# Decoder layer on one core: attention cut into two halves that run one batch apart, with the second recurrence of batch 0 ahead of the first of batch 1 in the prologue

## What is computed

```python
x = x + attn(layernorm(x))       # mix with the token before (tm_k, tm_v, tm_r); k, v, r = mixed @ Wk.T, Wv.T, Wr.T
                                 # out = (sigmoid(r) * layernorm(wkv(k, v))) @ Wo.T
x = x + wkv2(k=layernorm(x), v=ctx_2048)
x = x + ffn(layernorm(x))        # (silu(z @ gate.T * gs) * (z @ up.T * us)) @ down.T * ds, 1408 inner features
```

## Time and profile before

| | |
|---|---|
| time, median of 3 runs | 614.09 us (613.96 to 615.02) |
| time of the profiled execution | 616.2 us |
| its span in the trace | 614.2 us |
| busy: PE, DVE, ACT, POOL | 539.0, 460.5, 345.0, 47.9 us |
| granted clock of PE, mean | 0.945 |

### The profile page before, as it was taken

The page is one execution under the profiler, slowest core; times in us unless marked ns, Lnnn a source line. Parts: engine busy times, 40 slices in busy tenths (PEclk is TensorE's granted clock), DMA queues, the critical chain, the costliest instruction groups (busy, mean ns, idle before and its releaser), DMA issues.

```text
span 614.2 us, 8078 instructions
## 1 busy us (share of the span) xinstructions
PE 539.0 (88%) x2658; PEld 384.2 (63%) x2658; DVE 460.5 (75%) x727; ACT 345.0 (56%) x546; POOL 47.9 (8%) x155
## 2 busy tenths in 40 slices
PE   3998671269999997999999997999999997999995
PEld 2443331168447577997447477996447487999994
DVE  5899429928999459978999469968998479863343
ACT  4648447548546455758546365768556365763231
POOL 2000110012001110012001010012001010010000
PEclk9999695569999999999999998999999998999999
DMA  8999300010010000020020000030010000000001
GB/s 308 378 379 375 117 0 0 1 40 31 0 69 1 1 0 2 35 86 17 0 68 0 0 0 0 34 99 3 0 68 0 0 0 0 34 35 1 1 34 37
DMA packets 11877, 34.65 MB, mean 56 GB/s; under 512 B 912, under 2 KB 912, under 8 KB 11664
## 3 DMA queue, kind: packets, MB, share of 16 engines
q1 hardware_dynamic: 11856, 34.37, 15.3%
HBM read 30.18 MB, written 12.85 MB: 70 GB/s over the span
## 4 chain that ended last, share of the span: by engine, by line
PE 71%; DVE 12%; issue 6%; ACT 5%; POOL 2%; DMA 2%; SPq 0%; DVEq 0%; POOLq 0%; ACTq 0%
PE bank L473 27%; PE gu L557 19%; PE dacc L487 10%; PE bank L533 8%; PE bank L462 5%; DVE t_slot L773 2%; DMA t_xres<-in_x 2%; PE bank L510 1%; DVE t_stats L752 1%; DVE t_z L765 1%; POOL t_rstd L439 1%; ACT t_z L626 1%; DVE t_st L900 1%; ACT L580 1%; DVE t_slot L881 1%
## 5 line engine op out<-in xcount | busy, mean ns | idle before, releaser
L557 PE MATMUL gu<-t_z4h,t_gate 128*128 128x256 f32 x352 | 92.5, 294 | 15.0 <-DVE t_h L931 13.2
L557 PE MATMUL gu<-t_z4l,t_gate 128*128 128x256 f32 x352 | 90.5, 289 | 0.0
L557 PE MATMUL gu<-t_z4h,t_up 128*128 128x256 f32 x352 | 90.1, 288 | 0.0
L557 PE MATMUL gu<-t_z4l,t_up 128*128 128x256 f32 x352 | 89.9, 287 | 0.0
L557 PEld LDWEIGHTS gu<-t_z4h,t_gate 128*128 128x128 f32 x352 | 69.0, 196 | 19.1 <-DVE t_h L931 14.8
L697 ACT ACTIVATE t_h<-gu,t_fsc 128x256 f32<-128x256 f32 x88 | 40.2, 472 | 66.6 <-PE gu L557 62.1
L487 PE MATMUL dacc<-t_down,t_hh 128*128 128x512 f32 x176 | 73.3, 416 | 0.0
L557 PEld LDWEIGHTS gu<-t_z4l,t_gate 128*128 128x128 f32 x352 | 69.1, 196 | 0.9
L487 PE MATMUL dacc<-t_down,t_hl 128*128 128x512 f32 x176 | 69.5, 395 | 0.0
L557 PEld LDWEIGHTS gu<-t_z4h,t_up 128*128 128x128 f32 x352 | 68.9, 196 | 0.0
L557 PEld LDWEIGHTS gu<-t_z4l,t_up 128*128 128x128 f32 x352 | 68.8, 195 | 0.0
(11 more groups left out here) (110 smaller groups left out, 906.9 us busy)
## 6 DMA issues: line engine op xcount, KB each, us to landing
t_xres<-in_x SPq DMA_DIRECT2D x8, 512.0 KB, 3.9
t_mixv<-in_ctx_t SPq DMA_DIRECT2D x4, 1024.0 KB, 5.2
out<-t_otile SPq DMA_DIRECT2D x16, 256.0 KB, 2.0
gate_words<-in_gate_t SPq DMA_DIRECT2D x1, 2816.0 KB, 18.4
up_words<-in_up_t SPq DMA_DIRECT2D x1, 2816.0 KB, 24.4
t_gate<-gate_words SPq DMA_DIRECT2D x1, 2816.0 KB, 14.4
down_words<-in_down_t SPq DMA_DIRECT2D x1, 2816.0 KB, 21.6
t_up<-up_words SPq DMA_DIRECT2D x1, 2816.0 KB, 21.7
```

Source lines behind the costliest of these rows:

```text
L557: last = pe.matmul(gu[u % 2][:, side, :], as_read(w[:, k, i * P:(i + 1) * P], exact), as_read(part[:, k, hf * HALF:(hf + 1) * HALF], exact ...
```

## The change

The attention's steps are divided into those that run **ahead** (the first half above) and the others. In a round of the loop the engines now work on three batches: FFN of batch b-1, second half of batch b, first half of batch b+1. The loop has two rounds (b = 1, 2) in place of three. Around it:

- the prologue holds both halves of batch 0 and, marked with a `+`, the first half of batch 1. After `turn3` on PE and `norm5` on DVE the second recurrence of batch 0 comes first, and the recurrence of batch 1 behind it;
- a new list `..._NEXT` behind the loop holds the second half of batch 3 and the FFN of batch 2;
- `..._LAST` is, as before, the FFN of batch 3, in a slightly other order.

Tiles change so that two batches can be under way. x for the first half is loaded into `mixv` and normalised in place; the residual is loaded a second time, into `xres`. The context gets a tile of its own (two blocks of four, loaded in four pieces). The r mixture goes into `z` for batch 0, `xf` for batch 1 and `mixk` in the loop; in the last case ACT's `share_r0` waits until PE has finished `k3`. `rw` writes `tanh_r`, the second recurrence writes `z`, and the running maximum and the gap of `front` live in the slot, which costs one memset of one column per `front`. Statistics of the first normalisation have their own small tiles and semaphores. The four banks and the two slots are still used in turn, now in the order of the new lists. The sums that are computed are the same.

```diff
     PE_FIRST = """
-        turn1 k0 v0 k1 v1 k2 v2 k3 v3 r0 r1 r2 r3 turn2 return2 wo turn3 y turn4_0 flag
+        turn1 k0 k1 v0 v1 r0 k2 r1 k3 v2 v3 r2 r3 turn2 return2 wo turn3 turn1+ k0+ k1+ v0+ v1+ r0+ r1+
+        r2+ r3+ y k2+ k3+ flag v2+ turn4_0 v3+
         """.split()
     PE_BODY = """
...
+        up0 up1 up2 up3 turn4_1 up4 turn2 up5 down0 up6 up7 return2 down1 up8 down2 turn1 up9 down3 k0
+        k1 v0 v1 wo k2 k3 up10 down4 up11 down5 down6 v2 down7 up12 v3 r0 down8 r1 down9 down10 r2 turn3
...
     DVE_BODY = """
...
+        x1_3 part1 mixr0 fin0 mixr1 front2 fin1 prod10 mixr2 prod11 front3 nv2 mixr3 den2 num2 rest4
...
     SP_FIRST = """
-        ctxload
+        xload0+ words1 words2 xload1+ ctx2 ctx3
         """.split()
...
+    AHEAD = ("stat1_", "share_k", "share_v", "share_r", "mixk", "mixv", "mixr", "k", "v", "r", "front", "den", "nv",
+             "num", "part", "fin", "tanh", "xload")
+    AHEAD_ONE = ("rn0", "rn1", "norm0", "norm1", "turn1")
...
+        def mixr(b):
+            return {0: z, 1: xf}.get(b, mixk) if isinstance(b, int) else mixk
...
         def run_first(step, orders):
             for s in orders[0]:
-                step(s, 0, None)
+                step(s.rstrip("+"), int(s.endswith("+")), None)
         def run_rest(eng, step, orders):
-            with eng.Fori(1, B) as b:
+            with eng.Fori(1, B - 1) as b:
...
+                    elif lead(s):
+                        step(s, b + 1, None)
                     else:
                         step(s, b, None)
             for s in orders[2]:
                 if s in LATE:
+                    step(s, B - 2, None)
+                elif kind(s) in FFN_KINDS:
+                    step(s, None, B - 2)
+                else:
+                    step(s, B - 1, None)
+            for s in orders[3]:
...
             def load_x(b, hf):
-                need(sp, xf_done, b - 1, (hf + 1) * HB)
...
+                need(sp, newv_done, b - 1, C)
+                sp.dma_start(mixv[:, hf * HB:(hf + 1) * HB, :], rows_of(b, hf)).then_inc(x_in[hf], 16)
...
                 elif kind(s) == "share_r":
                     c = int(s[7:])
-                    need(act, zt_done, b, c + 1)
-                    share(TM_R, z, c, zt[:, c, :])
+                    if c == 0 and mixr(b) is mixk:
+                        need_filled(act, b, "k", C - 1)
+                    share(TM_R, mixr(b), c, zt[:, c, :])
```

More of the change, by code:

```diff
@@ L109, in decoder_layer @@
[L109 to L113 removed]
+        stat1_0 stat1_1 norm0 norm1 mixk0 mixk1 mixk2 mixk3 mixv0 mixv1 mixv2 mixv3 mixr0 mixr1 front0
@@ L120, in decoder_layer @@
-        den3 num3 part3 prod6 fin2 fin3 prod7 stat2_0 stat2_1 norm2 norm3 rw0 rw1 rw2 rw3 rest2 prod8
-        prod9 rest3 x1_0 x1_1 x1_2 x1_3 norm4 norm5 rest4 xfront0 xfront1 xin0 xden0 xnum0 prod10 prod11
-        xpart0 xin1 rest5 xden1 xnum1 prod12 prod13 xpart1 xfin0 xfront2 xfin1 rest6 xin2 xfront3 prod14
-        prod15 xden2 xnum2 out0 out1 xpart2 rest7 xin3 prod16 xden3 xnum3 prod17 prod18 xpart3 xfin2
-        xfin3 prod19 xf_0 xf_1 rest8 rest9 prod20 prod21 norm6 rest10 z4_0_0 z4_0_1 out2 out3
+        prod0 prod1 prod2 norm7 z4_1_0 z4_1_1 prod3 rest0 prod4 stat2_0 stat2_1 norm2 prod5 norm3 rest1
@@ new lines, in decoder_layer @@
+        xin2 xden2 xnum2 prod16 prod17 xpart2 rest7 xin3 xden3 xnum3 prod18 prod19 xpart3 xfin2 xfin3
+        rest8 xf_0 xf_1 prod20 prod21 rest9 rest10 norm6 z4_0_0 z4_0_1 out2 out3 xf_2 xf_3
+        """.split()
+    DVE_NEXT = """
+        prod0 prod1 norm7 prod2 prod3 z4_1_0 z4_1_1 rest0 prod4 stat2_0 stat2_1 norm2 norm3 rest1 prod5
+        rw0 rw1 rw2 rw3 prod6 prod7 x1_0 x1_1 norm4 rest2 x1_2 x1_3 norm5 prod8 prod9 xfront0 xfront1
+        xin0 xden0 xnum0 rest3 xpart0 prod10 xin1 xden1 xnum1 rest4 prod11 xpart1 xfin0 xfin1 prod12
+        prod13 rest5 xfront2 xfront3 out0 rest6 xin2 out1 xden2 xnum2 prod14 prod15 xpart2 xin3 xden3
+        prod16 rest7 xnum3 prod17 xpart3 xfin2 xfin3 prod18 prod19 xf_0 xf_1 rest8 rest9 prod20 prod21
+        norm6 rest10 z4_0_0 z4_0_1 out2 out3 xf_2 xf_3
@@ new lines, in decoder_layer, with lead, placed @@
+    AHEAD_ONE = ("rn0", "rn1", "norm0", "norm1", "turn1")
+    def lead(s):
+        if s in LATE or kind(s) in FFN_KINDS:
+            return -1
+        return int(kind(s) in AHEAD or s in AHEAD_ONE)
+    def placed(first, body, after, last, expand):
+        turns = [(u, int(s.endswith("+"))) for s in first for u in expand(s.rstrip("+"))]
+        rounds = [(u, lead(s)) for s in body for u in expand(s)]
+        for n in range(1, B - 1):
+            turns += [(u, n + ahead) for u, ahead in rounds]
+        turns += [(u, B - 1 + lead(s)) for s in after for u in expand(s)]
+        turns += [(u, B - 1) for s in last for u in expand(s)]
+        return turns, len(rounds)
```

439 lines of the change are left out of this document (272 added, 167 removed).

## The result

The changed kernel takes 609.35 us (median of 6 runs, 608.25 to 611.66). The kernel before took 614.43 us beside it (median of 6 runs). The ratio of the two times is 0.992, with an interval of 0.990 to 0.994: faster by 5.1 us, where 11 were forecast. The profiled execution took 608.74 us.

A forecast was written before the change was run, and what follows sets the result against it. PE, the busiest engine, was taken to bound the rounds, with waits and the prologue left to win. Prologue 167.5, two rounds 277.0, NEXT 89 and last stage 69.7 sum to a 603.2 us span, median 603.1; range 590 to 615.

The forecast's parts named there:

- The sign: Whole kernel: faster, median 603.1 us expected, with chance 0.83 of faster, 0.04 within 0.2%, 0.13 slower.
- The prologue: Before the first `up0`: 167.5 us against 130.59, +36.9, summed from DVE's work after the second recurrence starts at 93.3.
- The stall at `mixr0`: Loop round: DVE stands 5.7 us at its first r mixture, until `k3` ends and ACT may write the r share.
- a round gains nothing: Each of the two loop rounds takes 138.5 us, against a mean of 138.0 before.
- No PE wait over 0.4 us in the first 60 us: Early loop round: every PE input is in time, with no wait between 4 and 64.5 us.
- The stage NEXT: Stage behind the loop, without a first half: 89 us, between 86.2 and 93.7, set by the chain from `turn2` on.
- The conversion: From span to median: profiled execution 2.0 us over its span and 2.1 above the median, so 603.2 becomes 603.1.
- The pin: Loop round: DVE's list behind `mixr0` can't start before 65.2 us; 66.0 us of work then end `xf_1` at 131.2.
- the rival: Loop rounds: if DVE isn't held at `mixr0`, PE runs through at 128.8 + 1.7 us each, 587 in all; chance 0.10.
- PE's own work: Loop round: projections, `wo`, turns, up and down steps sum to 128.8 us on PE.
- waits of 9 to 10 us: Last third of a loop round: PE waits for `t_h` and `z4`, 9 to 10 us in sum.
- ACT's table: Loop round on ACT: 15 table loads against 13, 2.6 us more work, costed at nothing since ACT stands ready.

## Why the prediction was right, and where it failed

**Right.** The sign. The prologue: DVE has no gap over 0.52 us from the second recurrence on, 169.28 against 167.5. The stall at `mixr0`, 5.79 against 5.7. That a round gains nothing: the first took 137.0. No PE wait over 0.4 us in the first 60 us of it; in the second round two stood there, of 3.11 and 1.71 us, behind the jump. The stage NEXT, 88.55 against 89, is in part luck: the 89 was picked between 86.2 and 93.7, and PE was busy for 85.89 us of it.

**The miss, 6.25 us, by its terms.** A gain of 11 us was forecast and 5.1 were measured. Two steps of the prediction failed: the jump to the second round was priced at nothing, and the profiled execution was taken to lie as far above the median after the change as before. The stages give 3.7 of it: prologue +1.8, first round -1.5, second round +2.9, NEXT -0.4, last stage +0.9. The other 2.55 come from the step "the profiled execution took 2.0 us more than its span and lies 2.1 above the median", by which I took the median to be the span less 0.1.

- *The conversion.* After the change the time was 1.84 us over the span again, and the median 0.61 above the profiled execution. That one execution of the kernel before lay 2.1 us over its median doesn't carry over to the next kernel.
- *Prologue, +1.8.* "The second recurrence still starts on DVE at 93.3": it started at 94.54, behind batch 1's norm, which waited for POOL. The work from there on was 0.8 less than summed. And I had no term for the branch: the flag was written at 167.91, and `up0` followed 1.37 us later. The run with the flag earlier showed it. The rows of DVE:

```profile
94.07 0.55 DVE L988 TENSOR_SCALAR t_mixv<-t_mixv,t_rstd,t_nmr 128x512 f32<-128x512 f32 x1 [0.92 <-POOL t_nmr L585]
94.54 1.39 DVE L1073 SCALAR_TENSOR_TENSOR t_slot<-t_ramp,t_neg_wp,bank 128x512 f32<-128x512 f32 x2
...
167.79 0.12 DVE L1142 TENSOR_SCALAR t_general<-gu 1x1 int32<-1x1 f32 x1
```

- *Second round, +2.9.* "A round is then 138.5 us", and "Twice that is 277.0": I gave the jump no price, since in the kernel before it had none. It costs 2.55 us on DVE. At the second round's `mixr0` this made 3.5 us. The remaining 1.0 of the difference of 4.4 to the first round came behind the wait of 2.33 us at which the clock fell. Without the loop the span was 603.0, against the 603.2 that was summed, and the new order was worth 10.7 us. That the two spans agree so well is luck in part: written out, the prologue was 2.8 above its term and the two rounds together 2.9 below theirs.
- *The pin.* The number was right, and so was the sum of DVE's work behind it: `xf_1` ended 130.2 us into the first round, where 131.2 were summed. The reason was half right. "This pins all of its list behind" was the forecast's bound of a round, and the rival was that without it PE would run through at 130.5 us a round. With the pin taken away the round was 137.1: DVE then waited for PE's later steps instead, 1.37, 1.49 and 2.60 us. The stall alone doesn't set the round.
- *PE's own work.* 128.8 us were summed for a round. PE was busy for at least 130.1, at a clock of 1.00 (second round of the run with Wo in two parts). The floor of the rival was 1.3 too low. In the first round PE was idle for 5.8 us (137.0 less 131.2), where waits of 9 to 10 us were forecast for its last third.

**ACT's table.** The rows of ACT after the change show the next activation 1.29 us behind a load:

```profile
239.21 1.28 ACT L745 ACT_TABLE_LOAD   x1
240.50 0.84 ACT L879 ACTIVATE t_h<-gu,t_fsc 128x256 f32<-128x256 f32 x2
```

The two further loads per round were put at nothing, and no run took them out. The Trainium skill, ScalarE: Activation LUTs, section What ACT_TABLE_LOAD costs, puts a drain of about 1.38 us behind each load; this trace, with its 1.29 us from the start of a load of 1.28 to the next activation, doesn't agree.

## What to carry to other kernels

A stall of 6 us in the profile is no gain to be had until what comes next has been priced: write down when the following inputs would be there without it. In lists that are ordered by hand, an edit on one engine moves a wait to another through a bank, a tile or a later entry of a third list, and of ten such edits in the rounds none gave more than 2 us, while five cost 5 to 15. Give the loop's jump and the branch a term of their own, or a place among the rivals, and compare a forecast with several runs, since one execution lay 2 us off its median.
